# A hybrid layer's attention with the next batches' selective scans put into the same block

## The chip, the cores and the metric

The kernel runs on one core of one Trainium2 chip. The metric is the device time of one execution in microseconds (us), the median of a few executions. The profile is one further execution, recorded by the hardware profiler. The engines are TensorE (PE, with its weight loads shown as PEld), VectorE (DVE), ScalarE (ACT), GpSimd (POOL) and SyncE (SP, which here only issues transfers). Each engine works through its own list of instructions in order, and semaphores connect the lists.

## What is computed

The input `x` has 4 batches of 1024 tokens by 128 channels. All matrices stay in fp32 or in two fp16 parts of an fp32 value. In the reference, cut to what matters:

```python
# 1. selective state space, added to x
z = layernorm(x); x1 = z @ w1 + b; u = silu(conv3(x1)); v = silu(z @ v1 + b)
dt = softplus(u @ W_dt + b_dt); Bt = u @ W_B; Ct = u @ W_C            # 16 states
h = exp(dt * A) * h + dt * u * Bt ;  y = sum_n h * Ct                 # over 1024 tokens
x = x + ((y + u * D_skip) * v) @ w2 + b
# 2. mixture: one dense and two chosen of eight experts per batch, gelu, added to x
x = x + ffn(layernorm(x))
# 3. retention (8 columns of state per head, a scan over tokens), then softmax attention on
#    its output with 16 heads of 8 channels and l2-normed queries and keys, added to x
x = x + attention(retention(layernorm(x)))
# 4. the same ffn again
x = x + ffn(layernorm(x))
```

## The kernel before

The layer is a chain of stages. Each stage is one `Block`, in which every engine has its list, and a block ends when all engines have ended. `t.x_t` holds the 4 batches of `x`, channels by tokens, in SBUF from the first stage to the last. The order in `hybrid_layer` is: `load_constants`, `input_layernorms`, `scan_inputs` (makes u, v, dt, dt*u and the 16 rows of B and C of each batch), `selective_scan`, `ffn`, `retention`, `queries_and_keys`, `attention`, `ffn`, `store`. Every stage goes through the 4 batches, most of them in a hardware loop (`Fori`) whose body is one batch; the start of a stage and its end are not overlapped with any other stage.

**`selective_scan`** has 16 steps (states n) for each batch, all 1024 tokens wide. PE spreads row n of B over 128 partitions into `drive_ps` (two buffers) and row n of C into `c_ps` (one buffer). DVE multiplies B by dt*u (`drive`, L635), and scans with the decay (`scan`, L642). ACT makes the decay `exp(dt * a_n)` (L615) and copies C out of PSUM (L619). POOL multiplies state by C into `hc` (L685), and PE sums the `hc` with an identity matrix. DVE works in pairs: scan n-2, scan n-1, drive n, drive n+1.

Into this stage is also put the splitting of the eight experts' weights and of the dense weights into two fp16 parts, for the ffn to come. One split is: SP loads `w_raw` (L537, L538, one buffer); ACT scales it (`enlarge`, L602) after the copy of C in step n; ACT makes the high part (`high_part`, L607) after step n+1; POOL makes the low part (`low_part`, L677) after `hc` of step n+2; SP stores both parts (L540) and only then issues the loads of the next split. `SPLITS = (3, 11)` says in which steps n of each batch a split starts, so two for each batch. The list of SP for it is

```python
for k in range(2):
    sp.wait_ge(w_scaled.sem, w_scaled.before(b, k, 1))
    sp.dma_start(w_raw[:, 0, :], t.dram["w1e"][b * 2 + k]).then_inc(w_loaded, 16)
    sp.dma_start(w_raw[:, 1, :], t.dram["w2e"][b * 2 + k]).then_inc(w_loaded, 16)
    sp.wait_ge(w_low.sem, w_low.at(b, k))
    sp.dma_start(t.dram["w_split"][b * 2 + k], ...).then_inc(w_stored, 16)
```

and `enlarge` waits for `w_loaded` in ACT's list, so that the decays of the later steps stand behind that wait.

**`ffn`** makes 12 chunks for each batch (4 dense, 8 of two experts), with the layernorm and gate of the next batch in between. **`retention`** has 8 scans of 1024 tokens for each batch; it loads and splits its own weights at its start. **`queries_and_keys`** makes normed queries and keys.

**`attention`** takes 4 groups of 4 heads for each batch. A group has 16 units (2 halves of the queries by 8 chunks of the keys). For each unit PE makes 4 tiles of scores, 128 by 512, two to a buffer of `s_ps` (three buffers of 1024 columns); ACT takes the exponential of a buffer into `prob` (L1612); PE multiplies by the values into `o_ps` (L1584). Of each group DVE copies the sums out (L1651), SP moves rows of numerator and denominator to their channels (L1687), and DVE divides (reciprocal L1637, product L1642). At the end of a batch PE projects (L1559) and DVE adds to `x` (L1663).

## Time and profile before

| | us |
|---|---|
| median of 3 executions | 1412.36 (1409.70 to 1413.79) |
| profiled execution, its own time | 1414.99 |
| profiled execution, span from first to last instruction | 1413.2 |
| busy: PE, ACT, DVE, POOL | 1121.0, 990.6, 835.6, 325.5 |

The stages of the profiled execution, by their first and last instructions, are: loads and input layernorms to 30, `scan_inputs` to 96, `selective_scan` 96 to 346, `ffn` to 503, `retention` to 665, `queries_and_keys` to 729, `attention` to 1243, `ffn` to 1400, `store` to 1413. No engine is busy all the time: each stage has its own limit, and the time is the sum of the stages.

### The profile page before, as it was taken

The numbers are of one execution on the slowest core, as the hardware profiler recorded it, in microseconds if no ns is written. First come the engines' busy times: TensorE is split into PE (matmuls) and PEld (weight loads), VectorE is DVE, ScalarE is ACT, GpSimd is POOL, SyncE is SP. The second block draws the span as 40 slices with busy tenths as digits, with TensorE's granted clock in tenths as the row PEclk, the third lists the DMA queues.
The fourth block names the chain that finished last, engine by engine and source line by source line (L and its number), as shares of the span: only waits on it lengthen the run. The fifth ranks groups of instructions, "written<-read, shape, count | busy, mean of one in ns | idle before, by whom it ended". The sixth has DMA issues, their size and how long they took to land. (4 is left out here: it accounts for less than half of the span.)

```text
span 1413.2 us, 18871 instructions
## 1 busy us (share of the span) xinstructions
PE 1121.0 (79%) x5854; PEld 404.7 (29%) x5854; DVE 835.6 (59%) x1017; ACT 990.6 (70%) x1057; POOL 325.5 (23%) x194
## 2 busy tenths in 40 slices
PE   5748787776899956774539998898999889869996
PEld 3213333332444422321531111111111111124443
DVE  5879998996566559995850432324143232456664
ACT  3767665653788821222439999999999999848885
POOL 3127676765011025654000000000000000011110
PEclk8769999998999979898759999999999999969999
DMA  2000001000100000000010111111011111000001
GB/s 72 0 16 30 30 34 55 30 30 30 31 30 30 30 24 0 0 0 8 0 32 4 35 32 23 22 23 29 19 35 29 23 22 23 14 32 31 30 30 60
DMA packets 24182, 36.28 MB, mean 26 GB/s; under 512 B 7362, under 2 KB 11970, under 8 KB 24130
## 3 DMA queue, kind: packets, MB, share of 16 engines
q1 hardware_dynamic: 24130, 35.71, 9.3%
q8 instruction: 18, 0.29, 0.1%
q14 instruction: 34, 0.28, 0.1%
HBM read 16.82 MB, written 6.29 MB: 16 GB/s over the span
## 5 line engine op out<-in xcount | busy, mean ns | idle before, releaser
L1612 ACT ACTIVATE att_prob<-att_s_ps 128x1024 f32<-128x1024 f32 x512 | 470.8, 1436 | 11.0 <-PE att_s_ps L1574 11.0
L1584 PE MATMUL att_o_ps<-att_prob,att_va 128*32 128x512 f32 x2048 | 277.8, 616 | 2.0 <-ACT att_prob L1612 2.0
L1574 PE MATMUL att_s_ps<-att_q_st,att_k_st 32*128 32x512 f16 x1024 | 194.2, 393 | 49.7 <-ACT att_prob L1612 12.2
L685 POOL TENSOR_TENSOR scan_hc<-scan_state,scan_c_rep 128x1024 f32<-128x1024 f32 x64 | 151.9, 2391 | 71.1 <-DVE scan_state L642 70.8
L1637 DVE RECIPROCAL hv_h_seq<-hv_h_seq 32x1024 f32<-32x1024 f32 (+1 forms) x20 | 105.3, 5265 | 84.3 <-DMA hv_h_seq<-hv_h_seq 84.3
L787 POOL TENSOR_TENSOR ffn_veps<-ffn_mv,all_eps 128x4 f32<-128x4 f32 x16 | 9.1, 569 | 605.4 <-DVE ffn_mv L944 605.4
L642 DVE TENSOR_TENSOR_SCAN scan_state<-scan_decay,scan_drive_ps 128x1024 f32<-128x1024 f32 x64 | 142.9, 2270 | 0.3 <-ACT scan_decay L615 0.3
L1574 PEld LDWEIGHTS att_s_ps<-att_q_st,att_k_st 32*128 32x128 f16 x1024 | 47.0, 91 | 334.7 <-ACT att_prob L1612 315.6
L1651 DVE COPY hv_h_seq<-att_o_ps 128x512 f32<-128x512 f32 x32 | 22.1, 691 | 200.4 <-PE att_o_ps L1584 200.4
L282 PE MATMUL scan_y_ps<-scan_hc,all_ident 128*128 128x512 f32 x256 | 127.5, 622 | 8.6 <-DVE scan_y_sb L661 6.2
L619 ACT ACTIVATE scan_c_rep<-scan_c_ps 128x1024 f32<-128x1024 f32 x64 | 65.5, 1023 | 79.3 <-PE scan_c_ps L282 79.1
L1012 DVE SCALAR_TENSOR_TENSOR ffn_hid_lo<-ffn_hid,ffn_share,ffn_hid_hi 128x1024 f16<-128x1024 f32 x64 | 82.0, 1283 | 48.9 <-ACT ffn_hid_hi L920 48.3
L1318 POOL TENSOR_TENSOR ret_qm<-ret_mem,ret_q_sb 128x1024 f32<-128x1024 f32 x32 | 74.6, 2351 | 64.0 <-DVE ret_mem L1270 61.0
L916 ACT ACTIVATE ffn_hid<-ffn_h_ps,ffn_be 128x1024 f32<-128x1024 f32 x64 | 71.1, 1112 | 21.7 <-PE ffn_h_ps L292 18.6
L635 DVE TENSOR_TENSOR scan_drive_ps<-scan_drive_ps,ssm_du_t 128x1024 f32<-128x1024 f32 x64 | 77.7, 1220 | 13.8 <-PE scan_drive_ps L282 13.5
L282 PE MATMUL scan_drive_ps<-ssm_bc,ssm_sel 96*128 (+1 forms) x128 | 41.6, 408 | 48.1 <-DVE scan_state L642 37.6
L292 PE MATMUL ffn_o_ps<-ffn_hid_hi,ffn_w_sel 128*128 128x512 f16 x256 | 76.0, 379 | 2.2 <-DVE ffn_hid_lo L1012 2.2
L920 ACT ACTIVATE ffn_hid_hi<-ffn_hid,ffn_share 128x1024 f16<-128x1024 f32 x64 | 73.5, 1149 | 4.8
L292 PE MATMUL ffn_h_ps<-ffn_z_hi,ffn_w_sel 128*128 (+1 forms) x256 | 76.2, 379 | 0.0
L615 ACT ACTIVATE scan_decay<-scan_dt_b,scan_a_neg 128x1024 f32<-128x1024 f32 x64 | 73.0, 1140 | 0.1
L1270 DVE TENSOR_TENSOR_SCAN ret_mem<-ret_g_sb,ret_kv_ps 128x1024 f32<-128x1024 f32 x32 | 71.2, 2268 | 0.0
L1012 DVE SCALAR_TENSOR_TENSOR ffn_hid_lo<-ffn_hid,all_blend,ffn_hid_hi 128x1024 f16<-128x1024 f32 x32 | 42.9, 1341 | 44.3 <-ACT ffn_hid_hi L920 44.3
(216 smaller groups left out, 1536.8 us busy)
## 6 DMA issues: line engine op xcount, KB each, us to landing
ffn_w_sel<-w_split SPq DMA_DIRECT2D x16, 512.0 KB, 3.2
w_split<-scan_w_parts SPq DMA_DIRECT2D x8, 512.0 KB, 2.9
att_q_st<-hv_part SPq DMA_DIRECT2D x64, 64.0 KB, 2.1
att_k_st<-hv_part SPq DMA_DIRECT2D x64, 64.0 KB, 2.1
hv_h_seq<-hv_h_seq SPq DMA_DIRECT2D x96, 32.0 KB
ln_x_half<-in_x SPq DMA_DIRECT2D x8, 256.0 KB, 2.9
scan_w_raw<-in_w1e SPq DMA_DIRECT2D x8, 256.0 KB, 3.0
scan_w_raw<-in_w2e SPq DMA_DIRECT2D x8, 256.0 KB, 3.3
```

What stands on the lines that cost most here:

```text
L282: last = pe.matmul(out[:, h], w, rhs[:, h], start=start, stop=stop)
L292: last = pe.matmul(out[:, h], w, x[:, h], start=start and i == 0, stop=stop and i == len(parts) - 1)
L635: dve.tensor_tensor(drive_ps[n % 2][:, :], drive_ps[n % 2][:, :], t.du_t[:, b + n // NS, :], ALU.mult).then_inc(driven.sem, 1)
L642: dve.tensor_tensor_scan(state[:, k % 2, :], decay[:, k % 4, :], drive_ps[k % 2][:, :], 0.0, ALU.mult, ALU.add).then_inc(scanned.sem, 1)
L685: pool.tensor_tensor(hc[:, n % 4, :], state[:, n % 2, :], c_rep[:, n % 4, :], ALU.mult).then_inc(weighed.sem, 1)
L920: act.activation(hid_hi[:, m % 3, :], hid[:, m % 2, :], ACT.Copy, scale=weight_of_expert(k)).then_inc(casted.sem, 1)
L1012: dve.scalar_tensor_tensor(hid_lo[:, m % 3, :], hid[:, m % 2, :], weight_of_expert(m % M // FC), hid_hi[:, m % 3, :], ALU.mult, ALU.subtra ...
L1318: pool.tensor_tensor(qm[:, n, :], mem[:, n % 2, :], q_sb[:, :], ALU.mult).then_inc(weighed.sem, 1)
L1574: last = pe.matmul(s_ps[n % 3][:, i, :], k_st[rows, g % 2, kc * P:(kc + 1) * P], q_st[rows, g % 2, HALVES[half]], start=True, stop=True)
L1584: last = pe.matmul(o_ps[half][32 * j:32 * j + 32, :], va[:, g % 2, kc, j, :], prob[:, u % RING, j, :], start=kc == 0, stop=kc == KC - 1)
L1612: act.activation(prob[:, u % RING, 2 * pair:2 * pair + 2, :], s_ps[n % 3][:, :, :], ACT.Exp).then_inc(exped.sem, 1)
L1637: dve.reciprocal(den[mine, cols], den[mine, cols]).then_inc(recips.sem, 1)
```

## The change

The layer goes through the batches in two groups, (0, 1) and (2, 3).

* `selective_scan` runs for batches 0 and 1 alone, 32 steps. It still splits all nine sets of weights: `SPLITS` is now every third step, 1, 4, ..., 25, counted over both batches. SP's list has the same order as before.
* Then `ffn` on (0, 1); `retention` and `queries_and_keys` on (0, 1); `attention` on (0, 1) with the selective scans of (2, 3) in the same block; `ffn` on (2, 3, 0, 1); `retention`, `queries_and_keys` and `attention` on (2, 3); `ffn` on (2, 3); `store`. That is one `ffn`, one `retention`, one `queries_and_keys` and one `attention` block more.
* The scans in the attention block are cut in halves of 512 tokens, 64 steps in all, spread over the units by `steps_at`: about one step for every 1.7 units. In a step PE spreads B and C (`spread`), ACT makes the decay, DVE does drive, scan and the product with C, and POOL adds up y. `gate_y`, `lead_out` and `lead_in` finish a batch.
* `attention` has a new order: two buffers of `s_ps` instead of three. With scans beside it an exponential is 1024 columns as before; without, it is 1536 columns (`WIDE` 3). The division is done once for each batch on 128 partitions, in quarters, and no longer for each group on 32 partitions.
* All `Fori` loops outside the input layernorms and the store are unrolled; each stage clears its semaphores on POOL when it ends; weights of `retention` and constants of the later stages are loaded and split in `load_constants`; the copies `dt_b` and `h_b` are left out.

The core of the diff (loop heads and renamed operands are left out):

```diff
 def load_constants(t, whole):
...
+                sp.dma_start(w_all[:, 0:len(RET_MATS), :], d["ret_mats"]).then_inc(ret_loaded, 16)
+                sp.dma_start(w_all[:, len(RET_MATS):W, :], d["wsv"]).then_inc(ret_loaded, 16)
+                sp.dma_start(t.head_sum[:, :, :], d["head_sum"]).then_inc(att_loaded, 16)
...
+                act.activation(t.ret_hi[:, :, :], w_all[:, :, :], ACT.Copy, scale=WS).then_inc(ret_high, 1)
...
+                dve.scalar_tensor_tensor(t.ret_lo[:, :, :], w_all[:, :, :], WS, t.ret_hi[:, :, :], ALU.mult,
+                                         ALU.subtract)
...
 def selective_scan(t, batches):
-        SPLITS = (3, 11)
+        SPLITS = tuple(1 + 3 * k for k in range(E + 1))
...
+                for k in range(E):
+                    sp.wait_ge(w_scaled.sem, w_scaled.before(k, 0, 1))
+                    sp.dma_start(w_raw[:, 0, :], t.dram["w1e"][k]).then_inc(w_loaded, 16)
+                    sp.dma_start(w_raw[:, 1, :], t.dram["w2e"][k]).then_inc(w_loaded, 16)
+                    sp.wait_ge(w_low.sem, w_low.at(k))
+                    sp.dma_start(t.dram["w_split"][k],
+                                 w_parts[:, :, :, :].rearrange("p w h f -> p (w h f)")).then_inc(w_stored, 16)
...
+                for k in range(N * NS):
+                    b, n = divmod(k, NS)
+                    act.wait_ge(scanned.sem, scanned.before(b, n, 4))
+                    act.activation(decay[:, n % 4, :], t.dt_t[batches[b]][:, :], ACT.Exp,
+                                   scale=t.a_neg[:, n:n + 1]).then_inc(decayed.sem, 1)
...
+                    act.activation(c_rep[:, n % 4, :], c_ps[:, :], ACT.Copy).then_inc(c_copied.sem, 1)
+                    if k in SPLITS:
+                        enlarge(SPLITS.index(k))
+                    if k - 1 in SPLITS:
+                        m = SPLITS.index(k - 1)
+                        high_part(m, t.dense if m == E else w_parts)
...
 def attention(t, batches, following):
+    WIDE, BEHIND, RING = (2, 3, 12) if following else (3, 2, 15)
+    SCAN_FROM, SCAN_SPAN = (2, W + 4), (54, 54)
+    Y_AT, LEAD_AT, KEEP_AT = W - 4, W - 1, W
+    DIVIDE_AT, PROJECT_AT = W + 5, (W + 11, W + 13)
...
+                def spread(i, k):
+                    n, h = divmod(k, 2)
+                    if i and k == 0:
+                        pe.wait_ge(led_in.sem, led_in.at(i - 1, 1))
+                    pe.wait_ge(scanned.sem, scanned.before(i, k, 1))
+                    pe.matmul(b_ps[:, :], t.sel[:, n, :], t.bc[:, following[i], HALVES[h]], start=True,
+                              stop=True).then_inc(b_spread.sem, 1)
+                    pe.wait_ge(weighed.sem, weighed.before(i, k, 1))
+                    pe.matmul(c_ps[:, :], t.sel[:, NS + n, :], t.bc[:, following[i], HALVES[h]], start=True,
+                              stop=True).then_inc(c_spread.sem, 1)
...
+                def decays(i, k):
+                    n, h = divmod(k, 2)
+                    act.wait_ge(scanned.sem, scanned.before(i, k, 4))
+                    act.activation(decay[:, k % 4, :], t.dt_t[following[i]][:, HALVES[h]], ACT.Exp,
+                                   scale=t.a_neg[:, n:n + 1]).then_inc(decayed.sem, 1)
...
+                def divide(i):
+                    for n in range(4):
+                        cols = slice(n * 256, (n + 1) * 256)
+                        if n == 0:
+                            dve.wait_ge(moved, (i + 1) * G * MOVES)
+                        if n == 2:
+                            dve.wait_ge(last_moved, (i + 1) * MOVES)
+                        dve.reciprocal(den[:, cols], den[:, cols]).then_inc(inverted.sem, 1)
+                        dve.wait_ge(inverted.sem, inverted.at(i, n))
+                        dve.tensor_tensor(att[:, cols], num[:, cols], den[:, cols], ALU.mult).then_inc(normed.sem, 1)
...
 def hybrid_layer(nc, dram):
+            selective_scan(t, first)
+        t.v_tok = whole.sb("v_tok", [P, 2, TT, P])
+        t.part = whole.sb("part", [P, 2, 2, 2, T], F16)
+        ffn(t, "ffn1", first)
+        for batches, following in ((first, second), (second, [])):
+            with Stage(nc, f"hv{batches[0]}") as s:
+                t.h_seq = s.sb("h_seq", [P, 2, T])
+                retention(t, batches)
+                queries_and_keys(t, batches)
+            attention(t, batches, following)
+            ffn(t, f"ffn{batches[0] + 2}", following + batches)
         store(t)
```

## Rows read from the trace of the kernel before

**Rows 1.** Busy time by stage: window, length, busy us of each engine, clock, DMA.
```profile
96.10:148.80 52.70, 42.27 (x115) 16.41 (x116) 49.61 (x31) 39.16 (x40) 34.62 (x15) 0.86 0.10 30
...
208.40:269.30 60.90, 48.09 (x133) 19.34 (x132) 57.20 (x36) 37.70 (x38) 42.34 (x19) 0.94 0.10 34
...
739.60:1229.00 489.40, 443.35 (x3074) 90.39 (x3074) 149.72 (x86) 473.71 (x515) 0.00 (x0) 0.98 0.12 24
```

**Rows 2.** Timeline of ACT, scan stage: start us, length us, engine line, instruction.
```profile
149.92 1.15 ACT L615 ACTIVATE scan_decay<-scan_dt_b,scan_a_neg 128x1024 f32<-128x1024 f32 x1
...
270.40 1.15 ACT L615 ACTIVATE scan_decay<-scan_dt_b,scan_a_neg 128x1024 f32<-128x1024 f32 x1
```

**Rows 3.** Timeline of all engines around the first split, 96 to 142.
```profile
108.12 1.05 ACT L602 ACTIVATE scan_w_large<-scan_w_raw 128x1024 f32<-128x1024 f32 x1
109.06 1.14 ACT L615 ACTIVATE scan_decay<-scan_dt_b,scan_a_neg 128x1024 f32<-128x1024 f32 x1
...
112.67 1.05 ACT L607 ACTIVATE scan_w_parts<-scan_w_large 128x1024 f16<-128x1024 f32 x1
...
121.82 4.46 DVE L642 TENSOR_TENSOR_SCAN scan_state<-scan_decay,scan_drive_ps 128x1024 f32<-128x1024 f32 x2
...
124.18 4.67 POOL L685 TENSOR_TENSOR scan_hc<-scan_state,scan_c_rep 128x1024 f32<-128x1024 f32 x2
...
126.19 2.42 DVE L635 TENSOR_TENSOR scan_drive_ps<-scan_drive_ps,ssm_du_t 128x1024 f32<-128x1024 f32 x2
```

**Rows 4.** Timeline of all engines at the end of the scan stage.
```profile
328.50 2.13 POOL L677 TENSOR_TENSOR scan_w_parts<-scan_w_large,scan_w_parts 128x1024 f16<-128x1024 f32 x1
...
335.45 1.06 ACT L602 ACTIVATE scan_w_large<-scan_w_raw 128x1024 f32<-128x1024 f32 x1 [6.93 <-DMA scan_w_raw<-in_w2m]
...
344.75 1.28 DVE L665 SCALAR_TENSOR_TENSOR all_x_t<-scan_c_ps,all_vec,all_x_t 128x1024 f32<-128x1024 f32 x1 [3.88 <-PE scan_c_ps L282]
```

**Rows 5.** Timeline of all engines at the start of the program.
```profile
4.70 2.19 SPq L182 DMA_DIRECT2D ln_x_half<-in_x  x4
...
9.92 2.07 ACT L263 ACTIVATE all_x_t<-ln_tok_ps 128x512 f32 x4
```

**Rows 6.** Timeline in the first ffn: two batch starts, and its last instruction.
```profile
394.31 1.28 ACT L916 ACT_TABLE_LOAD   x1 [0.89 <-PE ffn_h_ps L292]
...
429.63 1.28 ACT L916 ACT_TABLE_LOAD   x1 [0.89 <-PE ffn_h_ps L292]
...
500.56 2.34 POOL L798 TENSOR_TENSOR all_x_t<-all_x_t,ffn_y 128x1024 f32<-128x1024 f32 x1 [27.09 <-DVE ffn_y L1006]
```

**Rows 7.** Timeline in the retention: weights, first scans of batches 0, 1, 3, end.
```profile
509.17 1.76 DVE L1254 SCALAR_TENSOR_TENSOR ret_w_lo<-ret_w_all,ret_w_hi 128x1536 f16<-128x1536 f32 x1 [0.91 <-ACT ret_w_hi L1206]
...
524.89 4.46 DVE L1270 TENSOR_TENSOR_SCAN ret_mem<-ret_g_sb,ret_kv_ps 128x1024 f32<-128x1024 f32 x2
...
560.71 4.46 DVE L1270 TENSOR_TENSOR_SCAN ret_mem<-ret_g_sb,ret_kv_ps 128x1024 f32<-128x1024 f32 x2
...
631.85 4.46 DVE L1270 TENSOR_TENSOR_SCAN ret_mem<-ret_g_sb,ret_kv_ps 128x1024 f32<-128x1024 f32 x2
...
664.22 1.02 ACT L1202 ACTIVATE hv_h_seq<-ret_h_ps 128x1024 f32<-128x1024 f32 x1 [22.01 <-PE ret_h_ps L1157]
```

**Rows 8.** Timeline in the attention: steady exponentials, a division, and the tail.
```profile
739.61 5.61 ACT L1612 ACTIVATE att_prob<-att_s_ps 128x1024 f32<-128x1024 f32 x6
...
837.01 6.54 DVE L1637 RECIPROCAL hv_h_seq<-hv_h_seq 32x1024 f32<-32x1024 f32 x1 [4.17 <-DMA hv_h_seq<-hv_h_seq]
...
892.44 89.94 ACT L1612 ACTIVATE att_prob<-att_s_ps 128x1024 f32<-128x1024 f32 x98 [2.59 <-PE att_s_ps L1574]
...
1213.49 16.45 ACT L1612 ACTIVATE att_prob<-att_s_ps 128x1024 f32<-128x1024 f32 x17
...
1231.13 0.69 DVE L1651 COPY hv_h_seq<-att_o_ps 128x512 f32<-128x512 f32 x1 [4.59 <-PE att_o_ps L1584]
...
1242.13 1.28 DVE L1663 SCALAR_TENSOR_TENSOR all_x_t<-att_s_ps,att_bias,all_x_t 128x1024 f32<-128x1024 f32 x1 [2.17 <-PE att_s_ps L1559]
```

More of the change, by code:

```diff
@@ L78, in __enter__ @@
     def __enter__(self):
+        self.sems = []
         return self
     def __exit__(self, *a):
+        nums = sorted(sem.num for sem in self.sems)
+        for first in (n for n in nums if n - 1 not in nums):
+            end = next(n for n in range(first, first + len(nums) + 1) if n not in nums)
+            self.nc.gpsimd.sem_clear(range(first, end))
         return self.ctx.__exit__(*a)
@@ L359, in _ @@
                 pe.wait_ge(wbc_ready, 32)
-                with pe.Fori(0, B - 1) as b:
+                for b in range(B - 1):
                     for_u(b + 1)
@@ L396, in _ @@
                 silus(0)
-                with act.Fori(0, B - 1) as b:
+                for b in range(B - 1):
                     copy_x1(b + 1)
@@ L765, in _ @@
             def _(sp):
-                with sp.Fori(0, B) as b:
+                for b in range(N):
                     sp.wait_ge(gate_steps.sem, gate_steps.at(b, 2))
@@ L1321, in _, with queries_and_keys @@
                 deviation(0)
[L1322 to L1327 removed]
+                for b in range(N):
+                    body(b, b == N - 1)
+def queries_and_keys(t, batches):
     nc, d = t.nc, t.dram
[L1331 to L1336 removed]
+    N = len(batches)
+    with Stage(nc, f"qk{batches[0]}") as q:
         raw = q.sb("raw", [P, 2, TT, P])
@@ L1389, in _ @@
                 project(0)
-                with pe.Fori(0, B - 1) as b:
-                    project(b + 1)
+                for b in range(N):
+                    if b + 1 < N:
+                        project(b + 1)
                     turn(b)
-                turn(B - 1)
             @block.scalar
@@ L1598, in _, with scores @@
-                pe.wait_ge(exped.sem, exped.at(B - 1, G * U * 2 - 1))
-                project(B, 0)
+                def scores(e):
+                    pe.wait_ge(exped.sem, exped.before(e, 0, 2))
+                    for n, tile in enumerate(tiles_of(e)):
+                        v, j = divmod(tile, GH)
+                        g, u = divmod(v, U)
+                        half, kc = divmod(u, KC)
+                        if u == 0 and j == 0:
+                            pe.wait_ge(stacked[g % 2], (g // 2 + 1) * STACK_MOVES)
+                        rows = slice(32 * j, 32 * j + 32)
+                        last = pe.matmul(s_ps[e % 2][:, n, :], k_st[rows, g % 2, kc * P:(kc + 1) * P],
+                                         q_st[rows, g % 2, HALVES[half]], start=True, stop=True)
+                    last.then_inc(scored.sem, 1)
@@ new lines, in _ @@
+                done = 0
+                for e in range(GROUPS + BEHIND):
+                    if e < GROUPS:
+                        scores(e)
+                    while done < V and group_of(GH * done + GH - 1) <= e - BEHIND:
+                        values(done)
+                        done += 1
+                    if e < GROUPS and (tiles_of(e)[-1] + 1) // GH > tiles_of(e)[0] // GH:
+                        v = tiles_of(e)[0] // GH
+                        for step in steps_at(v):
+                            spread(*step)
+                        for i in range(N - 1):
+                            if v == i * W + LEAD_AT and i < len(following):
+                                lead_out(i)
+                            if v - i * W in PROJECT_AT:
+                                project(i, PROJECT_AT.index(v - i * W))
@@ L1601, in _ @@
+                if len(following) == N:
+                    lead_out(N - 1)
+                for h in range(2):
+                    project(N - 1, h)
             @block.scalar
```

701 lines of the change are left out of this document (354 added, 347 removed).

## The prediction

> **What bounds the kernel now.** I read the page first: PE is busy 79% of the span, ACT 70%, DVE 59%, and no share says what a stage waits for. So the view to go by is the busy time by stage [rows 1]. In the scan stage DVE is busy 57.20 of 60.90 us for one batch and everything else is below it. In the attention ACT is busy 473.71 of 489.40 us, and DVE only 149.72. The change puts DVE's scans beside ACT's exponentials, so the reader should see that these two rows complement each other. Then I read the timelines of the stages, because each stage is entered and left with nothing beside it, and the change enters four stages more. The last thing was the order of the weight splits in the scan stage, where one engine's list waits for a transfer [rows 3, 4].
>
> **The scan stage.** It runs from 96.1 to 346.0 us, 250 us [rows 1, 4]. Batch 1 begins at 149.92 and batch 3 at 270.40 [rows 2]. A stage of two batches is the first and the last of them: (149.9 - 96.1) + (346.0 - 270.4) = 53.8 + 75.6 = 129 us. The change would then save 121 us here. But it also puts all nine splits into 32 steps, one every third step. In order, a split is: ACT enlarges in step n, POOL makes the low part after the product of step n+2, and only behind that does SP issue the next load, for which ACT waits in its list at step n+3, with the decay of step n+4 behind it. Rows give each link. From the end of a scan: product on POOL 2.33 us (half of 4.67) [rows 3], low part 2.13 us, and from its end at 330.63 to ACT's start on the loaded weights at 335.45, 4.82 us, which is SP's issues and the landing [rows 4]. From the start of that enlargement to the end of the next decay: 0.94 + 1.15 = 2.09 us [rows 3]. Now the cycle from one enlargement (S) to the next. If step n+1 is the first of DVE's pair, ACT has a copy and a high part before the next decay (0.93 each), so that decay ends at S + 5.0, scan n+2 (2.23) at S + 7.2, and the next enlargement starts at 7.2 + 2.33 + 2.13 + 4.82 = S + 16.5. If it is the second of the pair, scan n+1 ends at 4.3, two drives take 2.42 [rows 3], scan n+2 ends at 9.0, and the next starts at S + 18.3. The mean is 17.4 us. Undisturbed, a pair of steps is from 121.82 to 128.61, 6.7 us with the overlap, so three steps are 10.1 us. The split is thus the longer chain, by 7.3 us, and there are eight such intervals: +59 us. The work at the turn of a batch (60.9 - 16 x 3.35 = 7.3 us) can go into these waits in part; I take 4 us of it. The stage comes to 129 + 59 - 4 = 184 us, a saving of 66 instead of 121. The kernel before has 8 steps between its splits and shows no such wait except at the end, 6.93 us [rows 4]. Bounds: 176 (all of the turn hidden, 0.5 us faster landings) to 192.
>
> **The attention, first group.** The stage takes 514 us now. Entry to the first exponential is 10.6 us (729 to 739.61), and I keep it. 98 exponentials take 89.94 us, 0.918 each [rows 8], so 256 are 235 us. The three short breaks at each batch's turn (489.4 - 512 x 0.918 = 19 us over the stage) go away, because the order is rebuilt. The decays are new on ACT: 64 of 512 columns. Four copies of 512 columns take 2.07 us, 0.50 from start to start [rows 5], against 0.92 for 1024, so 512 columns are worth 0.42; a decay of 1024 is 1.04 from start to start, and a half is 0.63: 40 us. DVE's step is 0.69 (product from PSUM, as the copy of 512 [rows 8]) + 1.2 (scan, half of 2.23 and a start) + 0.69 = 2.6 to 2.7 us, 64 times 170 us, with copies, divisions and additions some 215 of 290 us: beside ACT's work. PE waits in `spread` for the former step's product. Steps are mostly 2 units apart (4.3 us), 20 times one unit (2.5 us), which is just met with the scores two buffers ahead; where a copy falls into it, PE stops: 4 us in all. The division of batch 0 is 8.1 us on DVE (6.54 us for 1024 columns [rows 8], a quarter each time with a product of 0.39) with steps behind it, of which some 5.5 us reach ACT. Projections and `lead_out` stop PE for about 3 us, the lost third buffer costs about 1.5. Together 14 us. With enough slack these are 0; I keep 40 as the upper end, 0.6 us for each of the 64 steps. The tail: 1.9 us from the last exponential (1229.94) to the end of the copy (1231.82); gate and `lead_out`, `lead_in` on DVE and PE about 4.9; the division, now all behind it, 8.1; projection and addition 1.8: 16.7 us, against 13.5 now (1229.94 to 1243.41). Sum: 10.6 + 235 + 40 + 14 + 17 = 317 us.
>
> **The second group.** 171 exponentials of 1536 columns at 0.918 + 0.42 = 1.34 us: 229 us. Entry 10.6, 2 us of stops, tail 14.2 (1.9, then 6.5 until all eight moves of the last half have landed, as 4.17 us are waited for four now [rows 8], half a division 4.0, and 1.8). 256 us. Both groups: 573, that is 58 more than now. The Trainium skill's page "ScalarE: Activation LUTs" (What ACT_TABLE_LOAD costs) gives an activation 186 ns and 0.833 ns for each element, with 93 ns overlapped by the next; by it a 1536-wide one would take 1.37 us and the sum would be 6 us more. No row here has a 1536-wide exponential, and the sum goes by the row.
>
> **One more ffn, retention, queries and keys.** A batch in the ffn is 429.63 - 394.31 = 35.3 us and the stage 502.9 - 346.0 = 156.9 [rows 4, 6], so entering and leaving costs 15.7 us; it happens once more, +15.7. Retention for two batches is: entry to the first scan 22.0 us less 2.7 for the weights that are now ready (0.91 wait and 1.76) , batch 0 560.71 - 524.89 = 35.8, and the last batch 665.2 - 631.9 = 33.4 [rows 7]: 88.5, twice 177 against 162.3 now, +14.7. Queries and keys: entries are shorter without table constants and `h_b`, and there is one more; I take 0, with 4 us to either side.
>
> **Start and clears.** The first transfer of `x` is issued at 4.70 us [rows 5]. Six more loads (about 0.45 us of issue each), landing, a high part of about 1.5 us and a low part of 1.76 us [rows 7] now stand before it: +6.7 us, an estimate. Clearing semaphores on POOL at the end of some 14 stages: no row shows one; between 0 and 3 us by POOL's smallest operations (0.2 us), I take 1.4.
>
> **The sum.** -66 + 58 + 15.7 + 14.7 + 6.7 + 1.4 = +30.5 us on a span of 1413.2, so 1443.7 for a profiled span, which with the 1.8 us around it is 1445.5. The profiled execution (1415.0) was 2.6 us above the median of the runs, so I state it from there: 1412.4 + 30.5 = 1443 us.
>
> **Rivals.** (1) *The splits don't hold up the scans* (the other side, faster). If the weights of the next split had landed when ACT comes to them, the stage would be 129 us: 1443 - 55 = 1388 us. It turns at one point: the loads would have to be issued about 7 us earlier than behind the low part. For it speaks only that the kernel before shows no wait between its splits; its distance is 8 steps. Against it is the 4.82 us row. (2) *The merged block is bound by the hand-over between DVE and PE.* PE issues the scores, and it stands in `spread` until DVE is done; if this stops ACT in every step by 0.6 us instead of in a few, the time is about 1443 + 38 - 10 = 1471 us. It decides if DVE needs more than about 3.1 us from the spread of B to the product; the row for 0.69 us and half a scan speak against, and the missing row for a 512-wide scan leaves it open. (3) *The unrolled loops give back more.* The ACT table load at 394.31 and 429.63 stands at the turn of a loop [rows 6]; if each turn of the other stages had some 1 us to give, as the attention's has, 12 turns give 12 us: 1431 us. The Trainium skill's page "Runtime: NRT & Kernel Launch" (Instruction fetch mechanics) says that a taken branch can force a fetch before execution goes on and that unrolling avoids it, which would be for this rival; no row that I read sets such a fetch apart from the other waits at a turn.
>
> **How the numbers follow.** The forecast as it stands 0.70, with its own range 1428 to 1462 (the bounds of the scan stage, of the stops in the first attention block, and of the small terms). Rival 1 0.08, rival 2 0.14, rival 3 0.08. The predicted time is that of the forecast. The range for 8 in 10 reaches to the middle of rival 2 and stops short of rival 1: 1420 to 1475. A change of under 0.3% (4 us) can't be told from none. Faster takes rival 1 and a little of the forecast's low end, 0.09; within 0.3% 0.04; slower 0.87.
>
> **What would show it.** In the profile after: (a) in the scan stage ACT waits for the transfer of `w_raw` before L602's successor some eight times, 5 to 8 us each, with DVE's scans idle; the stage ends near 285 us of the span and not near 230. (b) The first attention block lasts 305 to 330 us, ACT is busy over 90% of its middle, DVE about 70%. (c) The second lasts 250 to 262 us, its exponentials 1.34 us apart. (d) Three ffn stages, about 86, 157 and 86 us. (e) Two retentions of 88 us. The prediction is wrong if (a) is absent, or if in (b) PE waits for DVE's product in most steps.

## The result, and the profile after

The changed kernel takes 1457.33 us (median of 4 runs, 1455.68 to 1458.97) against 1412.57 in the same session; the ratio is 1.032, 95% interval 1.03 to 1.034. The prediction said 1443 with a range of 1420 to 1475 and slower with a chance of 0.87. The profiled execution has a span of 1456.8 us, 43.6 more than before, where the sum gave 30.5.

The stages, each from the end of the last instruction of the one before it to the end of its own last one (the first row ends, and the second begins, with PE's first spread of B):

| stage | before | after | difference | predicted |
|---|---|---|---|---|
| up to the first spread of the scan stage | 96.5 | 102.75 | +6.3 | +6.7 (and 1.4 for the clears) |
| selective scan stage | 249.6 | 201.2 | -48.4 | -66 |
| feed-forward, all | 313.6 | 85.4 + 153.0 + 85.4 | +10.1 | +15.7 |
| retention | 162.3 | 90.1 + 88.3 | +16.0 | +14.7 |
| queries and keys | 63.65 | 30.6 + 30.5 | -2.5 | 0 |
| attention | 514.5 | 322.1 + 254.7 | +62.3 | +58 |
| store | 13.0 | 12.8 | -0.2 | 0 |

The scan stage is the term that is off most, by 17.6 us; the feed-forward is off by 5.6 the other way. These are the windows of the changed kernel for it and for the two attention blocks (window, length, busy time of PE, PE weight loads, DVE, ACT and POOL with instructions, granted clock, DMA share, GB/s); they answer to [rows 1]:

```profile
102.75:303.95 201.20, 117.95 (x264) 43.75 (x264) 116.21 (x70) 83.19 (x83) 94.33 (x41) 0.77 0.13 45
510.00:832.10 322.10, 269.00 (x1680) 56.81 (x1680) 209.51 (x248) 280.19 (x321) 78.03 (x61) 0.94 0.10 21
1104.00:1358.60 254.60, 197.06 (x1544) 38.41 (x1544) 32.51 (x44) 230.99 (x172) 1.38 (x1) 0.95 0.12 26
```

In the first line no engine is busy for 60% of the time: the stage was DVE's before, at 57.20 of 60.90 us, and now it is nobody's. It looks like a chain through several engines, and the timelines below show one. In the second line ACT is busy 87% and DVE 65%: the merging does what the windows of before suggested. The third shows what is left of an attention without scans, DVE at 13%.

The page names the wait in the costliest groups (busy us and mean ns, then idle time of the engine just before, and what ended it):

```profile
L655 ACT ACTIVATE scan_w_large<-scan_w_raw 128x1024 f32<-128x1024 f32 x9 | 9.5, 1055 | 76.7 <-DMA scan_w_raw<-in_w2e 65.8
```

Nine enlargements of 1.06 us, and 76.7 us of ACT standing in front of them. Timeline of the changed kernel from one enlargement to the next (start, length, engine, line, instruction, idle time before it and what released it):

```profile
120.35 2.12 POOL L726 TENSOR_TENSOR scan_w_parts<-scan_w_large,scan_w_parts 128x1024 f16<-128x1024 f32 x1
...
122.50 0.35 SPq L597 DMA_DIRECT2D w_split<-scan_w_parts  x1
122.90 0.43 SPq L594 DMA_DIRECT2D scan_w_raw<-in_w1e  x1
123.37 0.78 SPq L595 DMA_DIRECT2D scan_w_raw<-in_w2e  x1
126.94 1.06 ACT L655 ACTIVATE scan_w_large<-scan_w_raw 128x1024 f32<-128x1024 f32 x1 [9.14 <-DMA scan_w_raw<-in_w2e]
127.90 1.13 ACT L665 ACTIVATE scan_decay<-early_dt_t,all_a_neg 128x1024 f32<-128x1024 f32 x1
128.94 1.00 ACT L669 ACTIVATE scan_c_rep<-scan_c_ps 128x1024 f32<-128x1024 f32 x1
129.12 2.29 DVE L691 TENSOR_TENSOR_SCAN scan_state<-scan_decay,scan_drive_ps 128x1024 f32<-128x1024 f32 x1 [6.78 <-ACT scan_decay L665]
...
130.00 1.03 PE L341 MATMUL scan_c_ps<-all_bc,all_sel 96*128 96x512 bf16 x2 [6.99 <-ACT scan_c_rep L669]
...
130.83 3.62 PE L341 MATMUL scan_y_ps<-scan_hc,all_ident 128*128 128x512 f32 x4
...
134.24 1.06 PE L341 MATMUL scan_drive_ps<-all_bc,all_sel 96*128 96x512 bf16 x2
...
135.34 1.23 DVE L684 TENSOR_TENSOR scan_drive_ps<-scan_drive_ps,early_du_t 128x1024 f32<-128x1024 f32 x1 [2.80 <-PE scan_drive_ps L341]
...
136.48 4.45 DVE L691 TENSOR_TENSOR_SCAN scan_state<-scan_decay,scan_drive_ps 128x1024 f32<-128x1024 f32 x2
...
147.64 1.06 ACT L655 ACTIVATE scan_w_large<-scan_w_raw 128x1024 f32<-128x1024 f32 x1 [10.85 <-DMA scan_w_raw<-in_w2e]
```

The predicted chain is there link by link: low part, SP's three issues, landing, enlargement 4.47 us after the end of the low part (4.82 in [rows 4]), decay, scan. The reader is to see one thing more, which the prediction does not have. PE stands 6.99 us for ACT's copy of C, because that copy is in ACT's list behind the enlargement. The y sum (3.62 us here, 1.88 once PE has been running again) and the next spread of B are in PE's list behind the spread of C, so DVE's second product is 2.80 us late. The nine enlargements start at 108.05, 126.94, 147.64, 164.00, 184.99, 201.34, 224.17, 247.34 and 267.61. Where the next step is the first of DVE's pair the intervals are 16.4 us twice (predicted 16.5), and 18.9 for the very first one; where it is the second they are 20.7, 21.0 and 20.3 (predicted 18.3). The two around the turn of the batch, one of each kind, are 22.8 and 23.2. All eight together are 159.6 us.

This is that turn:

```profile
214.27 1.20 DVE L704 TENSOR_TENSOR scan_yv<-scan_y_sb,early_v_t 128x1024 f32<-128x1024 f32 x1
...
224.17 1.06 ACT L655 ACTIVATE scan_w_large<-scan_w_raw 128x1024 f32<-128x1024 f32 x1 [12.64 <-DMA scan_w_raw<-in_w2e]
225.13 1.13 ACT L665 ACTIVATE scan_decay<-early_dt_t,all_a_neg 128x1024 f32<-128x1024 f32 x1
226.17 1.00 ACT L669 ACTIVATE scan_c_rep<-scan_c_ps 128x1024 f32<-128x1024 f32 x1
...
227.32 3.65 PE L341 MATMUL scan_c_ps<-scan_yv,all_mats 128*128 128x512 f32 x4 [10.15 <-ACT scan_c_rep L669]
...
231.44 1.23 DVE L684 TENSOR_TENSOR scan_drive_ps<-scan_drive_ps,early_du_t 128x1024 f32<-128x1024 f32 x1 [12.65 <-PE scan_drive_ps L341]
232.58 1.27 DVE L714 SCALAR_TENSOR_TENSOR all_x_t<-scan_c_ps,all_vec,all_x_t 128x1024 f32<-128x1024 f32 x1
```

The operand of the projection is ready at 215.47 and PE begins it at 227.32: it waits for the copy of step 20, which stands behind the enlargement of step 19. Work that I had counted as filling the wait comes after it.

Last, the first attention block, in the middle and behind the division of its first batch:

```profile
562.89 1.22 DVE L1711 TENSOR_TENSOR_SCAN att_state<-att_decay,att_b_ps 128x512 f32<-128x512 f32 x1
...
563.79 0.71 ACT L1645 ACTIVATE att_decay<-all_dt_t,all_a_neg 128x512 f32<-128x512 f32 x1
...
564.15 0.69 DVE L1718 TENSOR_TENSOR att_hc<-att_state,att_c_ps 128x512 f32<-128x512 f32 x1
...
564.40 3.84 ACT L1653 ACTIVATE att_prob<-att_s_ps 128x1024 f32<-128x1024 f32 x4
...
672.70 1.74 DVE L1691 RECIPROCAL att_den<-att_den 128x256 f32<-128x256 f32 x1
...
683.25 0.61 PE L1594 MATMUL att_b_ps<-all_bc,all_sel 96*128 96x512 bf16 x1 [6.80 <-DVE att_state L1711]
...
685.16 1.02 ACT L1653 ACTIVATE att_prob<-att_s_ps 128x1024 f32<-128x1024 f32 x1 [6.79 <-PE att_s_ps L1570]
```

A decay takes 0.61 us from start to start (563.79 to 564.40), a product 0.69, a scan of 512 columns 1.22: what the prediction worked out from wider rows. The four quarters of the division stand together on DVE, PE waits 6.80 us in its spread of B, and ACT 6.79 us for the scores behind it.

### The profile page after: what moved, and what is told of

It reads as the page before. It is cut to its first block and busy times, and to the rows that moved or that the text cites. A ratio compares the mean times of both kernels' runs of the same rounds, so it can differ in the third digit from the quotient of the medians.

```text
span 1456.8 us, 16373 instructions
## 1 busy us (share of the span) xinstructions
PE 1071.1 (74%) x5722; PEld 375.5 (26%) x5722; DVE 808.3 (55%) x1146; ACT 948.8 (65%) x959; POOL 325.6 (22%) x223
## 5 line engine op out<-in xcount | busy, mean ns | idle before, releaser
L1653 ACT ACTIVATE att_prob<-att_s_ps 128x1024 f32<-128x1024 f32 (+1 forms) x427 | 476.4, 1377 | 27.8 <-PE att_s_ps L1570 26.2
L1570 PE MATMUL att_s_ps<-att_q_st,att_k_st 32*128 32x512 f16 x1024 | 166.0, 392 | 78.6 <-ACT att_prob L1653 56.5
L1552 POOL TENSOR_TENSOR att_y<-att_y,att_hc 128x512 f32<-128x512 f32 x60 | 76.7, 1278 | 212.8 <-DVE att_hc L1718 212.8
L734 POOL TENSOR_TENSOR scan_hc<-scan_state,scan_c_rep 128x1024 f32<-128x1024 f32 x32 | 75.8, 2375 | 96.6 <-DVE scan_state L691 96.6
L691 DVE TENSOR_TENSOR_SCAN scan_state<-scan_decay,scan_drive_ps 128x1024 f32<-128x1024 f32 x32 | 72.1, 2275 | 43.8 <-ACT scan_decay L665 35.3
L1703 DVE TENSOR_TENSOR att_b_ps<-att_b_ps,all_du_t 128x512 f32<-128x512 f32 x64 | 44.6, 697 | 74.4 <-PE att_b_ps L1594 74.4
L341 PE MATMUL scan_y_ps<-scan_hc,all_ident 128*128 128x512 f32 x128 | 74.9, 719 | 3.9 <-POOL scan_hc L734 2.1
L966 ACT ACTIVATE ffn_hid_hi<-ffn_hid,ffn_share 128x1024 f16<-128x1024 f32 x64 | 73.5, 1149 | 5.9
L351 PE MATMUL ffn_h_ps<-ffn_z_hi,ffn_w_sel 128*128 128x512 f16 x256 | 76.2, 379 | 0.0
L847 POOL TENSOR_TENSOR all_x_t<-all_x_t,ffn_y 128x1024 f32<-128x1024 f32 x8 | 23.2, 2895 | 179.4 <-DVE ffn_y L1051 179.4
L341 PE MATMUL scan_c_ps<-all_bc,all_sel 96*128 96x512 bf16 x64 | 24.7, 476 | 50.7 <-ACT scan_c_rep L669 49.8
L655 ACT ACTIVATE scan_w_large<-scan_w_raw 128x1024 f32<-128x1024 f32 x9 | 9.5, 1055 | 76.7 <-DMA scan_w_raw<-in_w2e 65.8
```

The costliest lines, as they stand in the source:

```text
L341: last = pe.matmul(out[:, h], w, rhs[:, h], start=start, stop=stop)
L351: last = pe.matmul(out[:, h], w, x[:, h], start=start and i == 0, stop=stop and i == len(parts) - 1)
L691: dve.tensor_tensor_scan(state[:, k % 2, :], decay[:, k % 4, :], drive_ps[k % 2][:, :], 0.0, ALU.mult, ALU.add).then_inc(scanned.sem, 1)
L734: pool.tensor_tensor(hc[:, n % 4, :], state[:, n % 2, :], c_rep[:, n % 4, :], ALU.mult).then_inc(weighed.sem, 1)
L966: act.activation(hid_hi[:, m % 3, :], hid[:, m % 2, :], ACT.Copy, scale=weight_of_expert(k)).then_inc(casted.sem, 1)
L1552: pool.tensor_tensor(y[:, HALVES[h]], y[:, HALVES[h]], hc[:, k % 3, :], ALU.add).then_inc(summed.sem, 1)
```

## The experiments

Each time is a median and stands with its ratio to the kernel before on the same chip, but for the two kernels of runs 5 and 6, which leave work out and were profiled once. The stage lengths run from PE's first spread to the end of the last x addition; each is of one execution. Four kernels here have the same scan stage (the changed one and runs 5, 6 and 7), and it took 201.2, 198.6, 200.8 and 200.8 us, so a difference of 2 to 3 us in a stage says nothing.

**1. Loads issued early, one buffer each.** SP issues the loads for split k + 1 once ACT has enlarged split k, ahead of its wait for the low part of k.

```
 for k in range(E + 1):
     sp.wait_ge(w_scaled.sem, w_scaled.before(k, 0, 1))
     ...load split k (the last one is the dense weights)...
+    if k:
+        sp.wait_ge(w_low.sem, w_low.at(k - 1))
+        sp.dma_start(t.dram["w_split"][k - 1], ...)
-    sp.wait_ge(w_low.sem, w_low.at(k))
-    sp.dma_start(t.dram["w_split"][k], ...)
```

> Edit: the changed kernel, and SP issues the next split's two loads as soon as ACT has enlarged the former split (the raw buffer is free then), ahead of its wait for the low part. Theory (the chain low part, SP's issues, landing holds ACT up): ACT's waits on the transfer of w_raw, 6.5 to 12.6 us eight times now, go away. What is left is the chain without the load: from the end of scan n+2 product 2.33, low part 2.13, enlargement 0.94, decay 1.15, 6.5 us until scan n+4, against 4.65 undisturbed, so about 1.9 us for each of eight intervals: a stage of 129 + 15 = 144 us in place of 201, and a time near 1400 us (1388 to 1408). Rival A (the splits' own work in ACT's and POOL's lists is what costs): the stage stays above 185 us and the time above 1440. Rival B (the prediction's hand-over to SP is the whole stall, nothing else): 129 to 133 us, 1387.

Measured: 1413.42 us (ratio 1.0007 to before, 0.9989 to 1.0025), the stage 157.9 us. Rival A is out, and so is rival B, and the time lies above the range of the theory too. Of the 74 us that waiting costs (201.2 less the 127.7 of run 2), 43 went with the loads, not 57. What is left is in ACT's waits in this timeline:

```profile
121.63 1.06 ACT L654 ACTIVATE scan_w_large<-scan_w_raw 128x1024 f32<-128x1024 f32 x1 [4.50 <-POOL scan_w_parts L725]
...
124.69 0.77 PE L341 MATMUL scan_c_ps<-all_bc,all_sel 96*128 96x512 bf16 x2 [2.35 <-ACT scan_c_rep L668]
125.26 3.45 PE L341 MATMUL scan_y_ps<-scan_hc,all_ident 128*128 128x512 f32 x4
...
137.21 1.06 ACT L654 ACTIVATE scan_w_large<-scan_w_raw 128x1024 f32<-128x1024 f32 x1 [6.57 <-POOL scan_w_parts L725]
...
149.17 1.06 ACT L654 ACTIVATE scan_w_large<-scan_w_raw 128x1024 f32<-128x1024 f32 x1 [2.09 <-POOL scan_w_parts L725]
```

The wait now ends with the low part, and again PE's list passes it on: intervals of 12.0 us, as expected, alternate with intervals of 13.9 to 16 us, with 19.3 at the turn of the batch. My 1.9 us for each was right for the first kind only.

**2. Two buffers as well.** `w_large` and `w_parts` twice, used in turn, on top of the former edit.

> Edit: the run before this one, and two buffers each for the enlarged weights and for their parts, so that an enlargement waits neither for the former low part nor for its store. Theory: the 1.9 us for each interval that is left goes away too: a stage of 129 to 135 us, some 12 us less than with the early loads alone, a time near 1388 us. Rival A (the splits' own work costs): no change against the run before it, both above 1440. Rival B (nothing left to gain after the early loads): equal to the run before within 4 us.

Measured: 1382.16 us (ratio 0.9772, 0.9744 to 0.9801), the stage 127.7 us. Window of the stage:

```profile
100.75:228.45 127.70, 98.21 (x264) 38.23 (x264) 114.77 (x70) 83.52 (x83) 94.34 (x41) 0.91 0.21 70
```

The same 70 instructions of DVE and the same 9 splits, and DVE is busy 90% of it. So the splits' own work costs little (no run leaves the splits out), and waiting for them cost 73.5 us. It also gives the undisturbed stage, 127.7 us where I had 129. And the version is faster than both kernels, by 2.3% than the one before: what costs the changed kernel its gain is the order of its splits.

**3. and 4. The kernel before, with its splits three steps apart.** `SPLITS = (3, 6)`, and `(4, 7)`, in place of `(3, 11)`.

> Edit: the kernel BEFORE, with its two splits of a batch at steps 3 and 6 instead of 3 and 11; four close intervals, nothing else changed. Theory (a distance of three steps is too short for the chain through SP): from the end of scan 5 to scan 7 it is 2.33 + 2.13 + 4.82 + 0.94 + 1.15 = 11.4 us against 4.65, so +6.7 us for each of four, +27 us: 1439 us. Rival (the stall belongs to something else in the new block, as the merged batches or the unrolled lists): no change, 1412.

> Edit: the kernel BEFORE, with its splits at steps 4 and 7: four close intervals of the other parity, where the step behind an enlargement is the second of DVE's pair. Theory with the parity term seen in the changed kernel (20.8 us for such an interval, 16.4 for the other): about 4 us more for each of four than at steps 3 and 6, so +43 us, 1455 us. Rival (the parity has nothing to do with it, the longer intervals come from the turn of the batch): the same as at 3 and 6, 1439.

Measured: 1443.65 us (ratio 1.0206, 1.0175 to 1.0237) and 1448.36 (1.0244, 1.0207 to 1.028). Four close intervals alone, in a kernel without any of the rest, cost 31 and 36 us, 7.8 and 9.0 each. The stage alone is 282.8 and 284.7 us against 249.6, although the wait of 6.93 us at its end [rows 4] is gone in both. So a distance of three steps is enough to make the stall. The parity is a poor predictor: 1.2 us for each interval by the times, with ratios whose intervals overlap, and not the 4 that I wrote down. ACT waits 9.1 to 9.5 us in the one and 11.0 to 11.1 in the other. The waits of 6.5 and 6.6 us in the changed kernel all stand behind another close interval; that ACT then has no lead left to lose is my reading, which no run tests.

**5. to 7. What the first attention block is made of.** The second group's scans left out; the same with the decays kept; and 1024-wide exponentials in the second group's block too (`WIDE, BEHIND, RING = (2, 3, 12)` for both).

> Edit: the changed kernel with nothing of the second group's selective scan beside the first group's attention (it is left out, so x of batches 2 and 3 lacks the state-space part); the exponentials stay 1024 wide with the same buffers. The block lasts 322 us in the changed kernel, from 510 to 832 of its span. The prediction's sum for this form is 10.6 + 235 + 2 + about 16 = 264 us, 58 less. Rival (the merged work costs ACT nothing but its 40 us of decays, and something else makes the block long): 275 to 285 us.

> Edit: as the run before it, but ACT still computes the 64 decays of 512 columns at their places; the products, scans, spreads and sums stay left out. It tells ACT's own cost from the stops that DVE's and PE's steps make. The prediction's price, 0.63 us for each decay: 264 + 40 = 304 us, with 18 us left for stops and the scan's tail. Rival (a decay between exponentials costs more, up to 0.9 us, and the scan's steps stop nothing): 264 + 57 = 321 us, the whole block.

> Edit: the changed kernel with 1024-wide exponentials in the second group's attention too (two score tiles in place of three, the value products three groups behind, twelve probability tiles), nothing else. By the spacings in the changed kernel's trace, 256 x 0.918 = 235 us against 171 x 1.34 = 229 us, the wide form is worth 6 us: 1463 us. Rival (the wide form is worth nothing, as fewer and larger buffers stop ACT more): 1457. By the Trainium skill's page ScalarE: Activation LUTs (What ACT_TABLE_LOAD costs), 93 ns net for each instruction saved would make it 85 x 0.093 = 8 us.

Measured, from the start of the first exponential to the end of the last one: 241.9 us with nothing beside (512.72 to 754.65), 289.1 with the decays (514.39 to 803.53), 294.0 in the changed kernel (517.57 to 811.56). The whole block takes 266.0, 313.2 and 322.1 us. The merged scan costs 56 us in it, where I expected 58; the spans (1397.4, 1446.8 and 1456.8 us) differ by 59, but 4.9 of that lie ahead of the block, in stages that the edit leaves alone. The split of it between ACT and the rest was wrong. The decays alone bring 47.2 us, where I expected 40: 64 times 0.61 is 39, and the rest is in ten waits of up to 1.28 us, 11.3 us together against 2.2 with nothing beside. They are not the changed kernel's. The granted clock of the block is 0.93 here, 0.99 with nothing beside and 0.97 in the changed kernel, where PE has the spreads to do as well. In the timeline of the run with decays alone eight value products take 1.94 us in some places, at a granted clock of 0.50, and 1.06 in others, at 1.00, with the scores behind them:

```profile
548.16 1.94 PE L1585 MATMUL att_o_ps<-att_prob,att_va 128*32 128x512 f32 x8
...
553.27 0.61 PE L1570 MATMUL att_s_ps<-att_q_st,att_k_st 32*128 32x512 f16 x4
...
553.92 1.02 ACT L1652 ACTIVATE att_prob<-att_s_ps 128x1024 f32<-128x1024 f32 x1 [1.28 <-PE att_s_ps L1570]
...
583.45 1.06 PE L1585 MATMUL att_o_ps<-att_prob,att_va 128*32 128x512 f32 x8
```

Of such slow groups (1.57 to 1.94 us) the block has fourteen with the decays alone, two in the changed kernel and one with nothing beside. So run 6 does not give the share of the steps cleanly, and my plan for it was at fault. In the changed kernel the waits after the entry are 13.5 us: 8.2 of them right behind the division (6.79 and 1.38), 5.3 in sixteen others of at most 1.2. These are ACT's waits over the exponentials of the block, changed kernel first, then decays alone, then nothing beside (total, times, longest; the first 5.9 is the entry in each):

```profile
ACT att_prob L1653 <- PE att_s_ps L1570: 19.4, 19, 6.8
```

```profile
ACT att_prob L1652 <- PE att_s_ps L1570: 17.2, 11, 5.9
```

```profile
ACT att_prob L1653 <- PE att_s_ps L1570: 8.1, 5, 5.9
```

With nothing beside, 256 exponentials take 241.9 us, not 237: with two score buffers they are 0.936 us apart ((241.9 - 2.2) / 256), with three they were 0.918 [rows 8]. I put the 0.018 us down to the buffer; the two attentions differ in their order too, and no run changes the buffers alone. The same spacing shows in the second group's block: 1024 wide it takes 241.9 us, 1536 wide 230.6, and the time with the narrow form is 1467.49 (ratio to before 1.0385, 1.036 to 1.0409), 10 us over the changed kernel where I expected 6.

**8. The division in quarters at four units**, on top of the two buffers.

```
-if v == i * W + DIVIDE_AT:
-    divide(i)
+if i < N - 1 and v - i * W - DIVIDE_AT in (0, 1, 3, 5):
+    divide(i, ((0, 1, 3, 5).index(v - i * W - DIVIDE_AT),))
```

> Edit: the early loads and the two buffers (1382.2 us), and the division of the first batch of an attention block done in quarters at four different units (0, 1, 3 and 5 behind the place of now) in place of all four in one. In the changed kernel ACT waits 6.79 us for scores right behind the division and 1.2 and 1.4 us near it. Theory (DVE's 8.7 us of division hold up its scan steps, so PE in the spread of B, so the scores): with quarters of 2.2 us between the steps most of it goes, 5 to 8 us less, 1374 to 1377 us. Rival (DVE is short of time there in any order, or the projection then comes late and stops PE in place of it): no change, 1380 to 1384.

Measured: 1380.07 us (ratio 0.9767, 0.9741 to 0.9794), not to be told from 1382.16. The longest wait falls from 6.8 to 2.3 us, but all of them together only from 13.5 to 9.8: each quarter now makes a small one. The rival's number came out.

**9. One more feed-forward entry.** The middle stage of four batches as two stages of two.

> Edit: the changed kernel with its middle feed-forward stage, four batches, cut into two stages of two batches: one more entry and exit of a stage and nothing else. The prediction's price of an entry and exit is 15.7 us: 1457 + 16 = 1473 us. Rival (a stage's entry is cheaper in lists without loops, as the batch's turn is already 34.2 us in place of 35.3): 10 us or less, under 1467.

Measured: 1475.04 us (ratio to before 1.0443, 1.042 to 1.0467), 17.7 more than the changed kernel; from the first exponential of one attention block to that of the next it is 610.9 us against 593.9, +17.0.

**10. The spread of B one step ahead in PE's list.**

```
+if b == 0 and n == 0:
+    spread_b(b, n)
+if there(b, n + 1, NS, N):
+    spread_b(b, n + 1)
-if more:
-    spread_b(b, n)
 if more and n <= TAIL:
     spread_c(b, n)
```

> Edit: the changed kernel with PE's list in the scan stage in another order: the spread of B for step n+1 stands ahead of the spread of C for step n, which waits for ACT's copy. It tests why every second interval between two enlargements takes 20.7 to 21.0 us where the prediction's chain gives 18.3. Theory (PE's list in order: behind an enlargement ACT's copy is late, the spread of C waits for it, and the y sum and the next spread of B stand behind, so that DVE's second product is 2.5 us late): such intervals fall to about 18.3, the stage from 201 to 188 to 193 us, the time to 1444 to 1449. Rival (the 2.5 us come from matmuls at the lower clock, wherever they stand): the stage stays at 199 or more, 1455 to 1459.

Measured: 1451.49 us (ratio to before 1.0283, 1.0252 to 1.0315), the stage 195.5 us. The place where the gain should be has it. Enlargements in this timeline:

```profile
144.30 1.06 ACT L657 ACTIVATE scan_w_large<-scan_w_raw 128x1024 f32<-128x1024 f32 x1 [6.96 <-DMA scan_w_raw<-in_w2e]
...
148.83 1.03 PE L341 MATMUL scan_drive_ps<-all_bc,all_sel 96*128 96x512 bf16 x2 [8.24 <-DVE scan_state L693]
...
150.51 3.62 PE L341 MATMUL scan_y_ps<-scan_hc,all_ident 128*128 128x512 f32 x4
...
160.82 1.06 ACT L657 ACTIVATE scan_w_large<-scan_w_raw 128x1024 f32<-128x1024 f32 x1 [4.18 <-DMA scan_w_raw<-in_w2e]
...
179.07 1.06 ACT L657 ACTIVATE scan_w_large<-scan_w_raw 128x1024 f32<-128x1024 f32 x1 [7.11 <-DMA scan_w_raw<-in_w2e]
```

The intervals are 16.5 and 18.25 us, the prediction's 16.5 and 18.3, and the six ordinary ones together are 104.0 us, 9.6 less than in the changed kernel. The slow y sum of 3.62 us is still there and does no harm, so it is the order and not the clock. The whole fell short of what I expected by 3 us or more: the two intervals at the turn became longer, 23.2 and 25.5 us, since there the spread of B waits for a scan with the spread of C behind it, and the first enlargement comes 3.2 us later in the stage.

**11. That order in the kernel of run 8.**

> Edit: the run with the quarters and, with it, PE's other order in the scan stage. Theory: the order matters only where ACT stands still, and with loads in time it doesn't: the same as the run without it within 4 us, scan stage 127 us. Rival (PE's in-order list costs something in every pair of steps): the stage falls under 122 us, and the time by 5 us or more.

Measured: 1386.01 us (ratio 0.9824, 0.9792 to 0.9856), the stage 132.6 us, 5 us longer than without. Neither theory had that. In its timeline, at 113.02, PE stands 3.30 us in the spread of B for a scan, and the spread of C and ACT's copy come behind it. The order that helped the stalled stage hurt the running one.

**12. The turn of the batch.** The last three splits one step later.

```
-SPLITS = tuple(1 + 3 * k for k in range(E + 1))
+SPLITS = (1, 4, 7, 10, 13, 16, 20, 23, 26)
```

> Edit: the changed kernel with the last three splits one step later, at steps 20, 23 and 26 in place of 19, 22 and 25; nothing else. It tests why the two intervals around the turn of the batch take 22.8 and 23.2 us. In the changed kernel PE's projection at the turn waits 10.15 us for ACT's copy of step 20, and that copy stands behind the enlargement of step 19 and its wait of 12.64 us. With the enlargement behind that copy, theory: projection, x addition, next spread of C and copy (3.65 + 1.27 + 0.60 + 1.02 = 6.5 us) run beside the stall in place of after it, and one interval has a step more (3.35 us) under the same chain: 8 to 11 us less, 1446 to 1449 us. Rival (the turn's work is in series on DVE in any case): only the longer interval's 3.4 us, 1454 us, or nothing if another wait takes its place.

Measured: 1444.4 us (ratio to before 1.0234, 1.022 to 1.0248), 13 us less than the changed kernel, the stage 187.6. In the timeline the projection runs before the enlargement:

```profile
216.22 1.88 PE L341 MATMUL scan_c_ps<-scan_yv,all_mats 128*128 128x512 f32 x4
...
219.72 1.27 DVE L714 SCALAR_TENSOR_TENSOR all_x_t<-scan_c_ps,all_vec,all_x_t 128x1024 f32<-128x1024 f32 x1
...
222.07 1.06 ACT L655 ACTIVATE scan_w_large<-scan_w_raw 128x1024 f32<-128x1024 f32 x1 [6.34 <-DMA scan_w_raw<-in_w2e]
```

The rival's 3.4 us is out. One step's shift of three splits was worth 13.6 us of stage. The theory gives 3.35 of it to the step that the longer interval takes in, and leaves some 10 for the turn's work that now lies beside the stall. By the enlargements the gain is spread: the three intervals from the sixth on are 22.4, 20.8 and 16.3 us in place of 22.8, 23.2 and 20.3, and the stretch behind the last one is 30.3 in place of 36.3, one step shorter. The edit also moves the last splits from one kind of interval to the other, so the 10 is not the turn alone.

## Why the prediction was right, and what it mis-sized

**The splits hold the scans up: right.** Shown from both sides, by taking the stall away (runs 1 and 2) and by making it in the kernel before (3 and 4). Point (a) held in its mechanism; the waits are 6.5 to 12.6 us and not 5 to 8, and the stage ends at 303.95, not near 285. Rival 1 did not come true, but its figure is the price of the plan without the stall: 1388 predicted, 1382 measured in run 2. Its condition was too narrow: loads in time alone were not enough (1413 in run 1), since the single `w_large` is the next link.

**The term that was mis-sized is that stall**, 129 + 59 - 4 = 184 us against 201.2. The 129 is 127.7 in run 2. The 7.3 us for each interval is right for the chain that I wrote down: in run 10 six ordinary intervals add up to 103.95 us, where the same six of run 2 take 59.9, so 7.35 each. Two things are missing. PE's list in order hands the late copy on to the next spread of B: the same six intervals take 113.6 us in the changed kernel, 9.6 more than the chain. (The whole stage gains only 5.7 in run 10, as its turn and its start are longer.) And the "-4" for the turn has the wrong sign: the turn's work stands in the same lists behind the stall. The two intervals at the turn take 46.0 us against 25.6 in run 2, 20.4 more, where two times 7.35 less 4 is 10.7; run 12 gave back about as much by moving the splits. The sum is then 127.7 + 6 x 7.35 + 9.6 + 20.4 = 201.8, for 201.2 measured. Both are one error: I followed the chain that ends last and did not ask of each engine what stands behind the late instruction in its list.

**The first attention block: 322 against 317, with errors that partly cancel.** Entry 7.6 us, not 10.6: SP no longer issues the load of the output weights first, and ACT's table load of 1.28 us stands at the start of the block instead of just before the first exponential. Exponentials 239.7, not 235, where I had 1.5 for the lost third buffer. Decays 39, as predicted (40). Stops 13.5 (19.4 less the entry's 5.9), where I had 12.5 besides the buffer's share; 8.2 come from the division (I had 5.5), and 5.3 from everything else (I had 7). Another 1.8 us of the 294.0 is in no row that I can name. Tail 20.6, not 17: gate, `lead_out` and `lead_in` take 6.5 us (813.44 to 819.99) and not 4.9, and projection and addition 3.65 and not 1.8. Rival 2 is out: no stop of 0.6 us in each step, DVE at 65%.

**The second block: 254.7 against 256.** The 1536-wide exponential is 1.349 us with stops (230.63 / 171), close to what the row of the 512-wide copy gave (1.34). An estimate by the Trainium skill's page "ScalarE: Activation LUTs" (What ACT_TABLE_LOAD costs) was 1.37; the measurement lies between the two, nearer to the row.

**Feed-forward: +10.1, not +15.7.** An entry and exit costs 17.0 us (run 9), a little more than 15.7, as I had priced all four batches of a stage at 35.3 us. But in the changed kernel a batch takes 34.2 us. These are two batch ends in the middle stage, and behind them the one table load of that stage:

```profile
884.23 3.23 POOL L847 TENSOR_TENSOR all_x_t<-all_x_t,ffn_y 128x1024 f32<-128x1024 f32 x1 [19.82 <-DVE ffn_y L1051]
918.39 3.23 POOL L847 TENSOR_TENSOR all_x_t<-all_x_t,ffn_y 128x1024 f32<-128x1024 f32 x1 [19.44 <-DVE ffn_y L1051]
```

```profile
843.34 1.28 ACT L962 ACT_TABLE_LOAD   x1
```

Before, each of the three batches inside the hardware loop had a load of 1.28 us [rows 6], and the fourth, which stands behind the loop, had none; the batch ends stand 35.3 us apart over a turn with a load (400.70 to 436.02) and 34.3 over the one without (436.02 to 470.34). In the lists without loops only the stage's first batch has a load, and ACT does it while it waits for PE. So six loads are gone from the chain, at 1.0 to 1.2 us each: 6 to 7 us, and 17.0 less that is the +10.1. Rival 3 is right in the one place where its row was, and the retention, where ACT's and POOL's loops are gone too, shows nothing of it. Its first scans of the first two batches stand 35.82 us apart before [rows 7] and 35.81 in the changed kernel:

```profile
408.91 4.46 DVE L1287 TENSOR_TENSOR_SCAN ret_mem<-ret_g_sb,ret_kv_ps 128x1024 f32<-128x1024 f32 x2
...
444.72 4.45 DVE L1287 TENSOR_TENSOR_SCAN ret_mem<-ret_g_sb,ret_kv_ps 128x1024 f32<-128x1024 f32 x2
```

The Trainium skill's page "Runtime: NRT & Kernel Launch" (Instruction fetch mechanics) would have the gain in the branch. The traces show it in the table load: ahead of the batch's first gelu ACT stands 0.89 us at a turn of the loop and 0.83 at the turn behind it. No run here tells a fetch apart.

**The small terms.** Start +6.3 (6.7, and 1.4 for all clears). Retention 90.1 and 88.3 (88.5 each). Queries and keys -2.5 (0, bounds 4).

What stays open: the exact price of the scan's steps in the merged block, since run 6 changed PE's clock too; how much of the first block's exponentials the third buffer is worth; and why the 3.7 us of waits that run 8 took from ACT show only as 2.1 us, within the noise, in its time.

## What to carry to other kernels

When work that needs a transfer is packed closer, write down the cycle from one use of its buffer to the next, with every engine and queue in it, and compare it with the new distance; if it is longer, issue the load when the buffer is free and not when its result is done. Then ask of each engine what stands in its list behind the late instruction: a wait is not a gap that other work fills, unless that work is ahead of it in every list that it needs. A stage in which no engine is over 60% busy, where DVE ran at 90% with the same instructions in another version, had such a chain here.

## What the runs showed of the hardware

After PE had stood for 2.3 to 7 us, the four matmuls of a y sum took 3.45 to 3.62 us, and 1.88 a few us later. The windows of the two y sums of the changed kernel that are shown above and just behind it have a granted clock of 0.50 and 1.00, which are its two levels, 1.2 and 2.4 GHz:

```profile
130.83:134.45 3.62, 3.62 (x6) 1.29 (x5) 1.70 (x2) 3.04 (x4) 2.35 (x1) 0.50 0.00 0
135.57:137.45 1.88, 1.88 (x5) 0.56 (x3) 1.88 (x2) 1.02 (x1) 0.00 (x0) 1.00 0.00 0
```

The granted clock of the scan stage was 0.77 with the stalls and 0.91 without. Work added to ACT alone made PE slower: with the decays between the exponentials fourteen groups of value products ran at the lower level and held up ACT, and only two did in the changed kernel, where PE has the spreads to do as well (one execution of each). Exponentials of 1024 columns were 0.936 us apart with two score buffers and 0.918 with three, in two attentions that differ in their order as well. A scan of 512 columns took 1.22 us with a constant first value and 1.28 with a column of the former state as first value.
